# A two-layer graph kernel whose adjacency is turned by VectorE in 32x32 blocks, with half of the row sums added on GpSimd

## The chip, the cores and the metric

The kernel runs on one core of a Trainium2 chip, as one program on the five engines: TensorE (PE, with its weight loads as PEld), VectorE (DVE), ScalarE (ACT), GpSimd (POOL) and SyncE (SP), which here only starts transfers. The metric is the time of one execution on the device in microseconds, as the median of several runs. Everything is computed in fp32.

## What is computed

Two layers work on the same 4096x4096 matrix `adj` and on `x`, 4096x128. Reference, cut:

```python
h = maximum(layernorm(x), 0)
sens = exp(-(1/adj - 1)**2 / 0.5);  weights = where(adj < 1, sens, 0)
x = x + weights @ (h @ W0 + B)                     # layer 0, "acc0"
h = maximum(layernorm(x), 0)
A = adj + eye;  d = sum(A, axis=1) ** -0.5
x = x + relu(d[:, None] * A * d[None, :] @ (h @ W1.T))   # layer 1, "mix"
```

TensorE contracts over the partitions, so both products need the columns of `adj` on partitions, which is the transposed matrix. Layer 1 needs the finished x of all rows, so a block of `adj` whose columns are not known yet has to be stored and used later.

## The kernel before

`adj` is cut into 8 rows of 8 blocks of 512x512 (1 MiB each), 64 units in all. `G = 8` counts rows and columns, `T = 4` tiles of 128. Row by row, each unit goes through these steps (letters are used below):

- **a.** SP loads the block in `raw` (`load`, 4 buffers, one DMA over 128 partitions, runs of 2 KB).
- **b.** TensorE turns it by 16 transposes of 128x128 into PSUM (`turn_tile`, L364), ScalarE copies the result into `kept` in two halves (`copy_half`, L569), and SP stores `kept` in HBM (`store`) where a later use needs it.
- **c.** VectorE sums the raw rows (`row_sum`, L659, 2048 elements a partition).
- **d.** The weights: VectorE `cut` (L673: v*(v<1), one instruction whose two inputs are the same tile in SBUF), ScalarE `log` and `invert` (L574, L580, so that v becomes 1/v), VectorE `quad` (L680: (v-2)*v, again two inputs in SBUF), ScalarE `weigh` (L586: exp).
- **e.** TensorE `multiply_weights` (L381) adds four 128x512 products to `acc0`, three units behind the transposes (`MUL_LAG`).
- **f.** Layer 1: `mix_once` (L397) uses `kept` at once where the block's columns are known, `mix_late` (L420) takes a stored block that GpSimd has loaded back (`load_late`), and what is left comes in an end part (`mix_end_block`, L519, 17 blocks). One such product of a block is four matmuls of 512 columns, 8 records in the profile. Sums that don't fit into PSUM are added to `mixed` in SBUF by VectorE (`add_sum`).

After each row the small chain of that row follows inside the next one: `copy_x1t`, `turn_x1`, `make_x1`, `make_hid`, `turn_hid`, `copy_hid`, `multiply_support`, `make_support`. In the first row the messages (h @ W0 + B) are made between the units. The order on each engine is written out in `turn`, with loops over equal rows (`PHASES`), and the waits are semaphores on counts. The end part finishes eight output rows: `add_end`, `turn_out`, `finish`, a store.

## Time and profile before

| what | value |
|---|---|
| time of the runs | 651.94 us median of 3 (651.78 to 652.38) |
| profiled execution, span | 651.7 us |
| PE, PEld busy | 595.8 us, 337.1 us |
| DVE, ACT, POOL busy | 523.2 us, 479.0 us, 65.2 us |
| bytes moved by DMA | 157.67 MB, mean 242 GB/s |
| granted TensorE clock | 0.988 of full speed |

The span runs from the first to the last instruction of the profiled execution. Busy time is the union of an engine's instructions. An instruction's own duration is a little longer than the distance to the next start when instructions follow each other directly, since their ends overlap; the prediction counts with the distances.

### The profile page before, as it was taken

To read this page: it belongs to the slowest core of one execution; us is meant where nothing else is said; L and a number is where in the kernel's file an instruction comes from. 1 tells how busy PE (TensorE), PEld (TensorE's weight loads), DVE (VectorE), ACT (ScalarE), POOL (GpSimd) and SP (SyncE) were. 2 spreads that over 40 slices of the span, in tenths; PEclk is the share of its full clock that TensorE was granted. 3 is DMA by queue.
4 is the path that set the end of the run, shared out by engine and by line. 5 is a ranking of instruction groups with operands and counts; after the bars stand their busy time and mean duration, and the time that the engine had idled before them with its cause. 6 is when DMAs were issued, how large, how long until landed. Compare 5 with 4: busy or idle time off the path is not lost.

```text
span 651.7 us, 7163 instructions
## 1 busy us (share of the span) xinstructions
PE 595.8 (91%) x2307; PEld 337.1 (52%) x2307; DVE 523.2 (80%) x582; ACT 479.0 (73%) x357; POOL 65.2 (10%) x87
## 2 busy tenths in 40 slices
PE   2498988977979999999999999999999999999995
PEld 2475644544545555655555555554555554444432
DVE  4999999999999999999999994668763868531516
ACT  2799999999999999999999986476484665710000
POOL 2694000000000100010001000100000000001110
PEclk9799999999999999999999999999999999999999
DMA  9987685797886778677678883585744550527983
GB/s 258 388 322 252 236 293 194 263 313 261 271 284 229 253 264 303 252 237 266 223 272 312 300 337 130 186 283 194 268 168 152 202 221 0 205 83 301 301 295 104
DMA packets 54293, 157.67 MB, mean 242 GB/s; under 512 B 2561, under 2 KB 11010, under 8 KB 43778
## 3 DMA queue, kind: packets, MB, share of 16 engines
q1 hardware_dynamic: 48370, 114.43, 50.8%
q0 software_dynamic: 5904, 42.99, 18.0%
q8 instruction: 10, 0.16, 0.1%
q14 instruction: 9, 0.07, 0.0%
HBM read 112.33 MB, written 45.09 MB: 242 GB/s over the span
## 4 chain that ended last, share of the span: by engine, by line
PE 58%; DVE 22%; ACT 8%; issue 8%; DMA 3%; DVEq 0%; SPq 0%; ACTq 0%; POOL 0%; POOLq 0%
PE acc L381 18%; PE acc_late L420 11%; PE acc_once L397 11%; PE turned_ps L364 9%; PE turned_ps L519 6%; DVE rowpart L659 6%; DVE wt L680 5%; DVE wt L673 4%; DMA late<-adj_t_spill 3%; ACT wt L586 2%; PE side L420 2%; ACT wt L580 2%; ACT kept L569 2%; ACT wt L574 2%; DVE msg L779 1%
## 5 line engine op out<-in xcount | busy, mean ns | idle before, releaser
L381 PE MATMUL acc<-wt,msg 128*128 128x512 f32 x512 | 231.8, 596 | 20.4 <-ACT wt L586 20.4
L569 ACT COPY kept<-turned_ps 128x1024 f32<-128x1024 f32 x128 | 124.0, 1027 | 75.5 <-PE turned_ps L364 73.6
L680 DVE SCALAR_TENSOR_TENSOR wt<-wt 128x2048 f32<-128x2048 f32 x64 | 146.3, 2286 | 20.8 <-ACT wt L580 20.7
L381 PEld LDWEIGHTS acc<-wt,msg 128*128 128x128 f32 x512 | 93.8, 190 | 126.9 <-issue 101.9
L659 DVE TENSOR_REDUCE rowpart<-raw 128x4 f32<-128x2048 f32 x64 | 145.8, 2278 | 7.7 <-DMA raw<-in_adj_dram 7.7
L673 DVE SCALAR_TENSOR_TENSOR wt<-kept 128x2048 f32<-128x2048 f32 x64 | 146.2, 2284 | 5.0 <-ACT kept L569 5.0
L364 PEld LDWEIGHTS turned_ps<-ident,raw 128*128 128x128 f32 x1024 | 119.8, 144 | 36.7 <-issue 29.8
L364 PE MATMUL turned_ps<-ident,raw 128*128 128x128 f32 x1024 | 126.9, 279 | 9.6 <-DMA raw<-in_adj_dram 9.4
L586 ACT ACTIVATE wt<-wt 128x2048 f32<-128x2048 f32 x64 | 123.2, 1926 | 15.7 <-DVE wt L680 15.7
L574 ACT ACTIVATE wt<-wt 128x2048 f32<-128x2048 f32 x64 | 124.3, 1943 | 0.1
L580 ACT ACTIVATE wt<-wt 128x2048 f32<-128x2048 f32 x64 | 122.8, 1919 | 0.0
L397 PE MATMUL acc_once<-kept,support 128*128 128x512 f32 x184 | 82.8, 593 | 0.9 <-DVE support L750 0.9
L420 PE MATMUL acc_late<-late,support 128*128 128x512 f32 x160 | 71.7, 593 | 0.0
L519 PE MATMUL turned_ps<-late,support 128*128 128x512 f32 x136 | 61.2, 597 | 1.3 <-DMA late<-adj_t_spill 1.2
L397 PEld LDWEIGHTS acc_once<-kept,support 128*128 128x128 f32 x184 | 33.6, 190 | 37.6 <-issue 37.6
L420 PEld LDWEIGHTS acc_late<-late,support 128*128 128x128 f32 x160 | 29.6, 190 | 33.5 <-issue 33.5
L519 PEld LDWEIGHTS turned_ps<-late,support 128*128 128x128 f32 x136 | 24.8, 190 | 31.1 <-issue 26.3
L304 POOL TENSOR_SCALAR support<-x,mv 128x128 f32<-128x128 f32 x28 | 34.2, 1239 | 17.5 <-DVE support L769 17.5
L311 POOL COPY x<-x_now 128x512 f32 (+1 forms) x8 | 4.9, 612 | 299.1 <-DVE x_now L709 299.1
L835 DVE TENSOR_TENSOR mix_end<-turned_ps,mixed 128x512 f32<-128x512 f32 x8 | 5.5, 691 | 33.1 <-PE turned_ps L519 33.1
L319 POOL DMA_DIRECT2D late<-adj_t_spill x24 | 12.9, 536 | 176.5 <-PE acc_late L420 149.0
L702 DVE COPY x1t<-acc 128x512 f32<-128x512 f32 x8 | 5.5, 684 | 27.0 <-PE acc L381 27.0
(74 smaller groups left out, 216.2 us busy)
## 6 DMA issues: line engine op xcount, KB each, us to landing
raw<-in_adj_dram SPq DMA_DIRECT2D x64, 1024.0 KB, 5.7
adj_t_spill<-kept SPq DMA_DIRECT2D x41, 1024.0 KB, 7.1
late<-adj_t_spill POOLq DMA_DIRECT2D x41, 1024.0 KB, 5.3
x<-in_x_dram SPq DMA_DIRECT2D x4, 512.0 KB, 7.7
out_dram<-fin SPq DMA_DIRECT2D x8, 256.0 KB, 3.2
w_sb<-in_L_gnn_W_dram SPq DMA_DIRECT2D x2, 64.0 KB
b_row<-in_L_gnn_B_dram SPq DMA_DIRECT2D x1, 0.5 KB
```

The lines of the kernel that those rows point to most:

```text
L364: last = nc.tensor.transpose(turned_ps[:, q, a * P:(a + 1) * P], raw[:, p % RAW, a, q * P:(q + 1) * P], ident[:])
L381: mm = nc.tensor.matmul(acc0[:], msg[:, c * T + q, :], wt[:, p % WTS, q, :], start=(p % G == 0 and q == 0), stop=(p % G == G - 1 and q == ...
L397: mm = nc.tensor.matmul(acc_once[:], support[:, c * T + q, :], kept[:, p % KEPT, q, :], start=(begins and q == 0), stop=(ends and q == T - 1))
L420: mm = nc.tensor.matmul(acc[:], support[:, c * T + q, :], late[:, slot, q, :], start=(begins and q == 0), stop=(ends and q == T - 1))
L519: mm = nc.tensor.matmul(turned_ps[:, r % T, :], support[:, c * T + q, :], late[:, slot, q, :], start=((r, c) in begins and q == 0), stop=( ...
L569: nc.scalar.copy(kept[:, p % KEPT, q:q + 2, :], turned_ps[:, q:q + 2, :]).then_inc(copied, 1)
L574: nc.scalar.activation(v, v, ACT.Ln, bias=LN_GUARD).then_inc(ln_done, 1)
L580: nc.scalar.activation(v, v, ACT.Exp, scale=-1.0).then_inc(inv_done, 1)
L586: nc.scalar.activation(v, v, ACT.Exp, scale=-2.0, bias=-2.0).then_inc(wt_done, 1)
L659: nc.vector.tensor_reduce(rowpart[:, :, p:p + 1], raw[:, p % RAW], AX_X, ALU.add).then_inc(summed, 1)
L673: nc.vector.scalar_tensor_tensor(out=wt[:, p % WTS], in0=v, scalar=CUTOFF, in1=v, op0=ALU.is_lt, op1=ALU.mult).then_inc(cut_done, 1)
L680: nc.vector.scalar_tensor_tensor(out=v, in0=v, scalar=-2.0, in1=v, op0=ALU.add, op1=ALU.mult).then_inc(quad_done, 1)
```

## The change

All engine programs are written out over `u` = 0..63 units instead of loops over equal rows, and these parts differ:

- **Turning.** Units come in pairs: one `raw` buffer now holds 2 MiB (two neighbouring blocks), there are 2 buffers, and a pair is loaded by four DMAs of 32 partitions with runs of 1 KB, so that four 32-row groups of `adj` lie on the four quarters of the partitions. VectorE `transpose` turns 32x32 blocks in SBUF, straight from `raw` to `kept`. The 1024 TensorE transposes and the 128 copies of ScalarE go. x and out are read and written in the same permuted order, by DMAs of 32 partitions with runs of 512 B.
- **Row sums.** GpSimd adds the two halves of each run of a pair (`halve`, 2 inputs of 2048 elements a partition), VectorE sums the result, once per pair and not per unit (2048 elements). The parts of a row now lie on four partition quarters, and `sum_quads` (one small matmul) with `own_rows` (two small VectorE instructions) collects them.
- **Squares.** For two units of three ScalarE squares (`square`: (1/v-1)^2, bias -1), for each third (`u % 3 == 1`, 21 units) VectorE does `quad` as before.
- **Layer 1.** Eight PSUM banks are used: each row keeps its own sum in its bank, so the additions to `mixed` go (two rows are moved out by ScalarE in `evict`). 28 blocks are used at once, 20 late in the rows (`JOBS`: 1, 2, 3, 4, 5 and 5 in rows 2 to 7), 16 in the tail. 35 blocks are stored and loaded again where it was 41. In the tail the late blocks have 7 slots, not 3: the freed halves of `raw` serve too.
- **Places.** `copy_x1t` moves from VectorE to ScalarE. `make_x1` stands before the cut of unit 5 of a row, `make_support` before the cut of unit 7; the ScalarE copy that it needs is the last step of unit 6. `cut` follows its own unit's `turn`. `WTS` is 6.

The core of the diff (declarations, the first row's messages and the end are left out):

```diff
+def squared_by_dve(u):
+    return u % 3 == 1
...
+        adj_parts = adj.rearrange("(R e h i) (C q w) -> R h C q i e w", e=16, h=2, i=B, C=C4, q=Q)
...
+            def load(n):
+                g = n // C4
+                if n >= RAW:
+                    sp.wait_ge(halved, n - RAW + 1)
+                    sp.wait_ge(turned, 2 * (n - RAW + 1))
+                for q in range(Q):
+                    sp.dma_start(raw[q * B:(q + 1) * B, n % RAW],
+                                 adj_parts[g // 2, g % 2, col(2 * n) // 2, q]).then_inc(raw_loaded[n % RAW], 16)
...
+            load_x(0)
+            load(0)
...
+            load_x(1)
+            load(1)
+            load_x(2)
+            load_x(3)
+            for u in range(UNITS):
+                if spills(u):
+                    sp.wait_ge(turned, u + 1)
+                    store(u)
+                if u % 2 == 1 and u // 2 + RAW < PAIRS:
+                    load(u // 2 + RAW)
...
+            def halve(n):
+                pool.wait_ge(raw_loaded[n % RAW], 64 * (n // RAW + 1))
+                if n >= 1:
+                    pool.wait_ge(summed, n)
+                nc.gpsimd.tensor_tensor(halves[:], raw[:, n % RAW, :, 0:W // 2], raw[:, n % RAW, :, W // 2:W],
+                                        ALU.add).then_inc(halved, 1)
...
+            for n in range(PAIRS):
+                halve(n)
+                if n < C4 - 1:
+                    make_h0(n + 1)
+                for j in range(len(IN_TURN)):
+                    if load_pair(j) == n:
+                        load_late(j)
...
+            def square(u):
+                v = wt[:, u % WTS]
+                act.wait_ge(inv_done, u + 1)
+                nc.scalar.activation(v, v, ACT.Square, bias=-1.0).then_inc(square_done, 1)
...
+            for u in range(UNITS):
+                g, idx = u // G, u % G
+                log(u)
+                if u >= 1 and not squared_by_dve(u - 1):
+                    square(u - 1)
+                if g >= 1 and idx == 6:
+                    log_pows(g - 1)
+                invert(u)
+                if u >= 1:
+                    weigh(u - 1)
...
+                if g >= 1 and idx == 3:
+                    copy_x1t(g - 1)
...
+                if g >= 1 and idx == 6:
+                    exp_pows(g - 1)
+                    copy_hid(g - 1)
...
+            def turn(u):
+                n, h = u // 2, col(u) % 2
+                if u % 2 == 0:
+                    dve.wait_ge(raw_loaded[n % RAW], 64 * (n // RAW + 1))
...
+                dst = kept[:, u % KEPT].rearrange("p k (e i) -> p e k i", i=B)
+                src = raw[:, n % RAW].rearrange("p e (k h i) -> p e k h i", k=T, h=2)[:, :, :, h, :]
+                nc.vector.transpose(dst, src).then_inc(turned, 1)
+
+            def row_sum(n):
...
+                dve.wait_ge(halved, n + 1)
+                nc.vector.tensor_reduce(dst, src, AX_X, ALU.add).then_inc(summed, 1)
...
+            for u in range(UNITS):
+                g, idx = u // G, u % G
+                turn(u)
+                if g == 0:
+                    cut(u)
+                if idx % 2 == 1:
+                    row_sum(u // 2)
...
+                if g >= 1 and idx == 2:
+                    own_rows(g - 1)
+                if g >= 1 and idx == 5:
+                    make_x1(g - 1)
+                if g >= 1 and idx == 7:
+                    make_support(g - 1)
+                if g >= 1:
+                    cut(u)
+                if u >= 1 and squared_by_dve(u - 1):
+                    quad(u - 1)
```

## Rows read from the trace of the kernel before

**Rows 1.** The page, part 1: busy time of each engine

```profile
PE 595.8 (91%) x2307; PEld 337.1 (52%) x2307; DVE 523.2 (80%) x582; ACT 479.0 (73%) x357; POOL 65.2 (10%) x87
```

**Rows 2.** Windows: stretch and its length, then engines' busy time

```profile
core 0: us, PE busy (x) PEld busy (x) DVE busy (x) ACT busy (x) POOL busy (x), PEclk, DMA share, GB/s
60.00:120.00 60.00, 51.76 (x246) 32.27 (x245) 59.56 (x62) 58.00 (x45) 0.61 (x1) 1.00 0.75 259
360.00:450.00 90.00, 90.00 (x330) 49.15 (x329) 69.40 (x60) 63.87 (x46) 4.84 (x9) 1.00 0.65 233
560.00:651.70 91.70, 82.74 (x225) 37.70 (x223) 34.48 (x86) 11.57 (x9) 9.50 (x18) 0.99 0.64 223
```

**Rows 3.** The chain that ended last, in order of time: start, length, what

```profile
246.68 1.75 PE turned_ps L364 x16
248.43 3.44 PE acc_late L420 x8
...
612.12 8.17 DMA late<-adj_t_spill
```

**Rows 4.** Timeline of DVE: the sum that closes a row (3 of 8)

```profile
72.76 0.19 DVE L665 TENSOR_REDUCE pows<-rowpart 128x4 f32<-128x32 f32 x1
...
375.82 0.18 DVE L665 TENSOR_REDUCE pows<-rowpart 128x4 f32<-128x32 f32 x1
...
556.35 0.19 DVE L665 TENSOR_REDUCE pows<-rowpart 128x4 f32<-128x32 f32 x1
```

**Rows 5.** Timeline of DVE: start, length, instruction; large and small work

```profile
161.32 0.68 DVE L709 TENSOR_TENSOR x_now<-side,x 128x512 f32<-128x512 f32 x1
...
162.82 2.27 DVE L673 SCALAR_TENSOR_TENSOR wt<-kept 128x2048 f32<-128x2048 f32 x1
165.01 0.16 DVE L720 TENSOR_SCALAR pows<-pows 128x4 f32<-128x4 f32 x1
...
166.35 2.28 DVE L680 SCALAR_TENSOR_TENSOR wt<-wt 128x2048 f32<-128x2048 f32 x1
168.55 2.28 DVE L659 TENSOR_REDUCE rowpart<-raw 128x4 f32<-128x2048 f32 x1
170.75 2.28 DVE L673 SCALAR_TENSOR_TENSOR wt<-kept 128x2048 f32<-128x2048 f32 x1
172.95 0.15 DVE L733 TENSOR_TENSOR tmp<-inv 128x8 f32<-128x8 f32 x1
...
175.04 2.28 DVE L680 SCALAR_TENSOR_TENSOR wt<-wt 128x2048 f32<-128x2048 f32 x1
```

**Rows 6.** Timeline of ACT: two instructions that follow each other directly

```profile
304.10 1.92 ACT L574 ACTIVATE wt<-wt 128x2048 f32<-128x2048 f32 x1
305.91 1.91 ACT L586 ACTIVATE wt<-wt 128x2048 f32<-128x2048 f32 x1
```

**Rows 7.** POOL: ns min/median/max of a line; timeline (to 46.5, to 48.4); memsets

```profile
L304 POOL TENSOR_SCALAR support<-x,mv x28: 703/708/2907, 22.6 to 56.1; 128x128 f32<-128x128 f32 x28
44.18 2.91 POOL L304 TENSOR_SCALAR support<-x,mv 128x128 f32<-128x128 f32 x1
...
44.18 4.28 POOL L304 TENSOR_SCALAR support<-x,mv 128x128 f32<-128x128 f32 x3
...
44.23 2.28 DVE L680 SCALAR_TENSOR_TENSOR wt<-wt 128x2048 f32<-128x2048 f32 x1
L296 POOL MEMSET mixed<- 128x2048 f32 x1 | 1.8, 1797 | 0.0
L298 POOL MEMSET mixed<- 128x512 f32 x1 | 0.5, 517 | 0.0
```

**Rows 8.** Start: DVE's first instruction in the timeline, and a window

```profile
7.73 2.29 DVE L659 TENSOR_REDUCE rowpart<-raw 128x4 f32<-128x2048 f32 x1 [7.73 <-DMA raw<-in_adj_dram]
22.00:40.00 18.00, 11.12 (x57) 8.73 (x56) 17.90 (x19) 17.49 (x17) 17.36 (x15) 0.81 1.00 373
```

**Rows 9.** Timeline of DVE: the addition behind the last block

```profile
643.73 0.69 DVE L835 TENSOR_TENSOR mix_end<-turned_ps,mixed 128x512 f32<-128x512 f32 x1 [0.54 <-PE turned_ps L519]
```

More of the change, by code:

```diff
@@ L83 @@
-class Turn:
-    def __init__(self, first, w, known):
-        self.first, self.w, self.known = first, w, known
-        self.row = first + w
-    def blocks(self, p, per=1):
-        return (self.first * G + p) * per + self.w * (G * per)
-    def tally(self, events, p=0):
-        before = sum(sum(events(k)) * n for f, n, k in PHASES if f < self.first)
-        return before + self.w * sum(events(self.known)) + sum(events(self.known)[:p])
+C4 = 4
+Q = 4
+B = 32
+T = 4
+RAW, KEPT, WTS, LATE = 2, 4, 6, 3
@@ new lines, with col, at_once, spills @@
+LAG = 3
+PAIRS = G * C4
+UNITS = 2 * PAIRS
+ORDER = [[0, 1, 2, 3, 4, 5, 6, 7]]
+for turn_row in range(1, G):
+    young = turn_row - 1
+    ORDER.append([c for c in range(G) if c // 2 != young // 2] + [young ^ 1, young])
+def col(u):
+    return ORDER[u // G][u % G]
+def at_once(u):
+    return col(u) < u // G
+def spills(u):
+    return col(u) >= u // G and (u // G, col(u)) != (G - 1, G - 1)
+def spill_count(u):
+    return sum(spills(v) for v in range(u % KEPT, u + 1, KEPT))
+def once_count(u):
+    return sum(at_once(v) for v in range(u + 1))
@@ L178, in build @@
         inv_done = sem("inv_done")
+        square_done = sem("square_done")
         quad_done = sem("quad_done")
@@ L261, in turn @@
-            def turn(t, last=False):
-                for p in range(G):
-                    if not (last and p + AHEAD >= G):
-                        load(t, p + AHEAD, t.first * G + p + AHEAD)
-                    if stored(t.known)[p]:
-                        store(t, p)
-            sp.dma_start(w0_sb[:], w0).then_inc(w_loaded, 16)
-            sp.dma_start(w1_sb[:], w1).then_inc(w_loaded, 16)
-            sp.dma_start(b_row[:], b0.rearrange("(a d) -> a d", a=1)).then_inc(w_loaded, 16)
-            first = Turn(0, 0, 0)
@@ L289, in _ @@
+            for i in range(2):
+                sp.wait_ge(out_written[i], 64 * (G // 2))
         @block.gpsimd
@@ L536, in _ @@
[L536 to L552 removed]
+            ended = 0
@@ L614, in turn, with copy_hid @@
[L614 to L635 removed]
+            def copy_hid(g):
+                act.wait_ge(hid_turned, g + 1)
+                nc.scalar.copy(hid_t[:], side[:]).then_inc(hid_t_done, 1)
@@ L648, in _ @@
+            square(UNITS - 1)
+            weigh(UNITS - 1)
+            copy_x1t(G - 1)
             log_pows(G - 1)
@@ new lines, in make_quads @@
+            def make_quads():
+                dve.wait_ge(ident_done, 1)
+                quads = ident[:].rearrange("p (q i) -> p q i", q=Q)
+                for q in range(Q):
+                    nc.vector.tensor_reduce(quad_sum[:, q], ident[:].rearrange("p (q i) -> p i q", q=Q), AX_X, ALU.add)
+                for a in range(T):
+                    for c in range(C4):
+                        last = nc.vector.tensor_reduce(own_quad[:, a, :, c:c + 1], quads, AX_X, ALU.add)
+                last.then_inc(quads_done, 2)
@@ L838, in finish @@
[L838 to L853 removed]
+            take_moments(0)
@@ new lines, in _, with finish @@
+            own_rows(G - 1)
+            make_x1(G - 1)
+            make_support(G - 1)
+            def finish(i):
+                r = ENDS[i]
+                rows = slice(r * T, r * T + T)
+                dve.wait_ge(mix_turned, i + 1)
+                if i >= 2:
+                    dve.wait_ge(out_written[i % 2], 64 * (i // 2))
+                nc.vector.tensor_tensor(fin[i % 2], tail_bank[r][:].rearrange("p (a d) -> p a d", a=T),
+                                        support[:, rows, :], ALU.add).then_inc(out_summed, 1)
+                dve.wait_ge(out_summed, i + 1)
+                for a in range(T):
+                    last = nc.vector.tensor_scalar(fin[i % 2][:, a, :], fin[i % 2][:, a, :],
```

902 lines of the change are left out of this document (394 added, 508 removed), and 10 rows, old and new, of tables (JOBS, LATE).

## The prediction

> **What bounds the kernel now.** I read the busy times of the page first. TensorE is busy for 91% of the span, VectorE for 80%, ScalarE for 73% [rows 1]. Shares over a whole span hide the stages, so I read the windows next. In the stretch 60 to 120 VectorE is busy 59.6 of 60 us, ScalarE 58.0 and TensorE 51.8; from 360 to 450 TensorE alone is full, and behind 560 the others have little left [rows 2]. So there are two regimes. The row ends show them in time: five rows from 72.76 to 375.82 take 303.1 us, 60.6 each; what follows takes 275.9 us to the end of the span [rows 4]. In the first regime VectorE and ScalarE set the pace together, in the second TensorE does, with its blocks following each other at 3.44 us and the turns at 1.75 us [rows 3]. The chain also has waits for late blocks in the tail, two of about 8 us, of which one is shown [rows 3].
>
> The reader should see what follows from that: removing TensorE work pays from row 6 on, and only there. In rows 1 to 5 the turns are not on the bound of TensorE, but their replacement is put on VectorE, which has nothing free.
>
> **TensorE, rows 6, 7 and tail.** Removed: 64 turns of 1.75 us, 112 us in all, though only those behind 375.82 are on the path [rows 3]. What stays from the start of row 6: 8 weight blocks, 6 at once, 5 late; then 8, 7 and 5; then 3 and 16. That is 19 + 20 + 19 = 58 blocks, and 58 x 3.44 = 199.5 us. Three small chains add two groups of four transposes and four products each, at the transposes' pace (1.75 for 16) some 2 us a chain: 6. Eight output turns at the same pace and a wait each, 3.5. The last weights come late by ScalarE's work on the last unit: I allow 5 us. Behind the last block stand the addition, an output turn, the finish and the store as now; that takes from 643.7 to 651.7, 8.0 us [rows 9]. Sum 222 us, against 275.9 now. The two late-block waits of 8 us are gone in it, since 7 slots let loads run ahead: a block of 1.05 MB at the 373 GB/s of a full window takes 2.8 us [rows 8], less than the 3.44 it serves. If that cover fails, up to 16 us come back.
>
> **VectorE, rows 1 to 5.** Large instructions of 2048 elements start 2.20 us apart: 166.35, 168.55, 170.75, 172.95 [rows 5]. Before, a row has 8 sums, 8 cuts and 8 quads. After, it has 8 turns, 8 cuts, 4 sums and 21/8 quads: 22.6 x 2.20 = 49.8 us, not 52.8. The trace has no VectorE transpose. Its nearest rows are the one-input sum and the two-input cut, both with 2048 elements and both at 2.28 us [rows 5]; one pass at 2.20 is what I take. Below that I see no case, since no instruction of this size is faster. The other bound is two passes, 4.4 us.
>
> Small work: the three stretches 161.32 to 162.82, 165.01 to 166.35 and 172.95 to 175.04 sum to 4.9 us [rows 5] and stay. The copy and the additions go; `own_rows` (0.5) and the wait of each cut for the turn right ahead of it (0.5) come: 5.9.
>
> A new wait: `make_support` now stands before the cut of unit 7, and needs the last step of ScalarE's unit 6. After the cut of unit 6 ScalarE has log, square, invert and weigh, 4 x 1.81 [rows 6], two small activations and the copy, about 8.3; TensorE's products take 1 more. VectorE has only a turn, a sum and 1 us of small steps, 5.4. It waits some 3.5 us a row, with unit 7's cut behind it and ScalarE's next log behind that. Together 49.8 + 5.9 + 3.5 = 59.2 us a row, about what it is now (60.6): two thirds of the squares have paid for the turns. ScalarE, at 29.4 activations a row by 1.81 and 2 us of small ones, has 55, and is not the bound. TensorE has as few as 9 blocks in row 1, and the granted clock was 0.81 where it was busy 11.1 of 18 us [rows 8]; even at the lower of its two levels, 1.2 GHz, 9 blocks take 62 us, so this costs nothing there.
>
> **GpSimd's additions.** This decides. In the trace GpSimd's short instruction takes 703 ns as a rule and 2907 at most; the one at 44.18 needs 2.91 us, and stands beside VectorE's two-input quad of 44.23 to 46.51 [rows 7]. So they use something together, and GpSimd waited. The trace has no long GpSimd instruction, so the opposite, a cut waiting for an addition, is not shown. The addition's own time is unknown too. A memset passes an element in (1797 - 517) / 1536 = 0.83 ns [rows 7]. If its three streams (two in, one out) all overlap, the addition takes 1.8 us; if they follow each other, 5.2. I take 4.3, between two and three streams one after another. (The 703 ns for 128 elements, scaled, would give 11 us, but the memset of 512 takes 517, so most of it is fixed.)
>
> The placement: `halve(n)` starts when the sum of pair n-1 is done. Beside it the cut starts first; the addition follows, and runs through the next turn, which has one input. After 2.3 us comes the next cut and has to wait 2.0 us. For the pair of unit 1 `own_rows` hides 0.5: 1.5. At unit 5 `make_x1` (about 3.7 us with its waits) leaves 0.6. At unit 7 it lies in the 3.5 us above. Where a quad follows the cut, in one pair of three, it may lose 4.3 instead of 2.0: 0.7 a row. Together 4.8, so a row takes 64.0 us and five take 320. Bounds: 0 if the addition takes under 2.3 us, and 7.8 a row at 5.2 us.
>
> The Trainium skill (SBUF — State Buffer, Who interferes with whom) says that a VectorE instruction with two SBUF inputs and a GpSimd instruction that reads SBUF exclude each other for the whole instruction, and that the later one blocks fully. The row at 44.18 agrees for GpSimd as the later one. With that rule the sum is the one made here, without it the first rival's. The same notes (GPSIMD Engine Reference, Elementwise — side-by-side cycle accounting) measured 4497 ns for such an addition; by it a row would be 0.7 us longer, and the sum 4 us.
>
> POOL's queue also holds `make_h0` and the late loads. A late load waits for a block that TensorE finished some five units earlier, so it doesn't hold the next `halve`.
>
> **Row 0.** Before, VectorE starts at 7.73 with one MiB landed [rows 8]. After, 1 MiB of x and 2 MiB of a pair come first: at 373 GB/s 5.6 us more than one block, 13.3; at half that rate 22. I take 15. From 7.73 to 72.76 were 65.0 us with 22 large instructions; there are 22 again (8 turns, 8 cuts, 4 sums, 2 quads). The messages stay. Added: 20 small reductions of `make_quads` 5, GpSimd's additions 4 x 2.0 = 8, the last cut 2. Row 0 ends at 95; now about 75.
>
> **Sum.** 95 + 320 + 222 = 637. In rows 5 to 7 VectorE (64), and TensorE (17, 19 and 20 blocks, 60 to 71 us) are close to each other, and where two paces meet both lose a little: 2 us a row, 6. **643 us**. The span of 651.7 is 0.2 under the median of the runs, 651.94, so nothing is added. About 49 us are won behind row 5 and about 39 lost before. What lies within 0.2% (1.3 us) can't be told from no change.
>
> **Rivals.**
>
> 1. *GpSimd doesn't hold VectorE up* (the addition is short, or only GpSimd ever waits). Rows of 59.2, row 0 at 87: 87 + 296 + 222 + 6 = **611**. For it: the only blocked engine in the trace is GpSimd. Against it: a thing used by two is seldom given back in the middle.
>
> 2. *The loads become the bound; slower.* A DMA now reaches 32 partitions in place of 128, with runs half as long. A row moves 15 MiB: at 373 GB/s 42 us, hidden. If the 8.39 MB of raw go at half that rate, 44.9 + 19.7 = 64.6 us a row, level with VectorE, and with two buffers only both wait for each other; at 5% more a row is 68. Then 20 more in rows 1 to 5, 8 in row 0 and 4 behind: **675**. It decides where raw falls under some 185 GB/s. Against it: the trace has no DMA of 32 partitions. The Trainium skill (SBUF — State Buffer, Door 1: The DMA port swizzle) says that 32 partitions reach 8 of 16 ports and measured 189 GB/s; a row would take 64.1 us by it, so it speaks for this rival. No row here shows it.
>
> 3. *The addition stops all of VectorE*, turns too: three pairs a row lose 4.3 and not 1.6. Rows of 72, also in rows 6 and 7; 105 + 360 + 227 + 6 = **698**. Against it: behind the quad, beside VectorE's one-input sum, GpSimd's next two took (4.28 - 2.91) / 2 = 0.7 us each, undisturbed [rows 7].
>
> 4. *The turn takes two passes.* 59.2 + 17.6 = 77 a row, over GpSimd's addition and over TensorE in all of rows 1 to 7: 105 + 539 + a tail of 84 = **728**.
>
> **How the numbers follow.** The forecast's case 0.45, its own range 625 to 662 (addition from 3.5 to 5.2 us, first load from 13 to 22): 0.28 of it faster, 0.05 the same, 0.12 slower. Rival 1 0.25, faster. Rival 2 0.17, rival 3 0.07, rival 4 0.06, all slower. Faster 0.53, same 0.05, slower 0.42. The range 604 to 692 leaves out rivals 3 and 4 and the edges of the rest.
>
> **What the profile after would show.** The turn at 2.3 us by 64. GpSimd's addition at 4 to 5 us by 32, and cuts behind it of 4 us where the rest take 2.3; only 2.3 everywhere means rival 1. A wait of VectorE for TensorE's products of some 3 us a row at `make_support`. Waits for `raw` on VectorE's turn only in row 0; in every pair they mean rival 2. Row ends 64 us apart until row 5, then 68 to 73. TensorE busy about 470 us. What would make it wrong most easily is the two-engine conflict, worth 32 us between its ends, and the loads.

## The result, and the profile after

The changed kernel takes **693.84 us** (median of 4 runs, 688.3 to 694.83) against 651.86 for the kernel before on the same chip: ratio 1.063, 95% interval 1.059 to 1.067. It is slower by 42 us; the forecast was 643, a gain of 1.4%, and its range ended at 692.

The page, part 1 answers to [rows 1]. TensorE lost 79 us of work, VectorE gained 14, GpSimd 147; nobody is above 78%:

```profile
PE 516.6 (75%) x1299; PEld 245.0 (35%) x1299; DVE 537.4 (78%) x579; ACT 450.9 (65%) x294; POOL 212.6 (31%) x98
```

The windows answer to [rows 2]. The first is row 1 (without its first turn, which starts at 94.7), the second rows 2 to 5 (without row 5's last quad), the third rows 6 and 7, the last the tail:

```profile
core 0: us, PE busy (x) PEld busy (x) DVE busy (x) ACT busy (x) POOL busy (x), PEclk, DMA share, GB/s
97.00:172.00 75.00, 35.02 (x83) 15.99 (x82) 64.20 (x49) 49.91 (x31) 23.99 (x8) 0.78 1.00 266
172.00:459.00 287.00, 217.41 (x508) 99.33 (x507) 245.84 (x196) 219.82 (x134) 91.91 (x24) 0.86 0.84 213
459.00:607.00 148.00, 142.16 (x352) 63.78 (x352) 119.77 (x99) 109.56 (x68) 45.06 (x18) 0.99 0.67 178
607.00:693.00 86.00, 78.36 (x220) 37.02 (x218) 24.99 (x77) 16.02 (x16) 6.83 (x13) 0.97 0.52 183
```

Before, VectorE was busy 59.6 of 60 us in the matching stage [rows 2]. Now it is busy 245.8 of 287, ScalarE 219.8 and TensorE 217.4: **no engine is full in rows 2 to 5**. Behind row 5 TensorE is full, as forecast. To size the stages I take the start of `make_support` (L757), which the timeline gives once a row. Two of the eight close the stages:

```profile
168.91 1.13 DVE L757 TENSOR_SCALAR support<-side,scale 128x128 f32<-128x128 f32 x4
...
455.69 1.13 DVE L757 TENSOR_SCALAR support<-side,scale 128x128 f32<-128x128 f32 x4 [1.84 <-PE side L443]
```

I put it 3.4 us ahead of a row's end, so the forecast's sum reads 95 + 64 - 3.4 = 155.6, then 4 x 64 = 256, then 231.4. (It is 3.2 in row 1 and 5.4 in row 5, where a quad follows; with these two the last column reads 13, 33 and 4.)

| stage (by L757) | forecast | measured | off by |
|---|---|---|---|
| start to row 1 | 155.6 | 168.9 | +13 |
| rows 2 to 5 | 256.0 | 286.8 | +31 |
| row 6 to the end | 231.4 | 237.3 | +6 |

Where does VectorE stand still in rows 2 to 5? The waits of DVE in 172 to 459 (us in total, times, longest), and what ScalarE waits for there:

```profile
DVE tmp L661 <- ACT inv L570: 15.6, 4, 5.8
DVE x L729 <- PE side L431: 14.6, 4, 5.9
DVE wt L657 <- ACT wt L530: 5.3, 4, 1.6
DVE support L757 <- PE side L443: 4.2, 3, 1.8
...
ACT wt L525 <- DVE wt L651: 76.3, 15, 16.6
```

VectorE waits 39.7 us for ScalarE and TensorE, 9.9 a row. ScalarE waits 76.3 for VectorE; of this the longest wait, 16.6, began in row 1 at 155.6, so some 60 belong to rows 2 to 5, 15 a row. Each waits for the other. The chain of waits around one row shows how (start, length, what):

```profile
271.63 1.91 ACT wt L525
273.54 1.80 ACT wt L535
275.34 1.80 ACT wt L530
277.14 1.80 ACT wt L544
278.94 0.48 ACT x1t L562
...
279.56 6.39 PE acc L393 x8
285.95 0.45 PE side L431 x4
286.42 0.70 DVE x L729
...
289.50 2.19 DVE wt L651
```

A cut ends, ScalarE does four large steps and the small copy, TensorE a weight block and four transposes, and only then can VectorE begin `make_x1`, 14.8 us after the chain's start. The next cut is queued behind `make_x1` and starts at 289.50, 17.9 us after the chain's start, and ScalarE's next logarithm waits 5.1 us for it. Beside the chain VectorE does two turns, a cut and a sum, to 282.5; then it stands still for the 3.9 us that are left. TensorE's block takes 6.39 us there. Timeline of PE, and the window of that block (granted clock 0.57, near the lower level of 1.2 GHz, behind 11.1 us of idling):

```profile
279.56 6.39 PE L393 MATMUL acc<-wt,msg 128*128 128x512 f32 x8 [11.10 <-ACT x1t L562]
...
286.22 3.60 PE L393 MATMUL acc<-wt,msg 128*128 128x512 f32 x8
```

```profile
279.50:286.00 6.50, 6.44 (x10) 2.85 (x11) 3.04 (x2) 6.50 (x4) 3.32 (x1) 0.57 1.06 359
```

The next block takes 3.60 us, at a granted clock of 1.00 (286.2 to 289.8).

The second loss is the read conflict. Timeline of DVE (answers to [rows 5]) and of POOL, around one addition:

```profile
199.02 2.28 DVE L651 SCALAR_TENSOR_TENSOR wt<-kept 128x2048 f32<-128x2048 f32 x1
201.21 2.31 DVE L635 STREAM_TRANSPOSE kept<-raw 128x2048 f32<-128x2048 f32 x1
203.55 4.29 DVE L651 SCALAR_TENSOR_TENSOR wt<-kept 128x2048 f32<-128x2048 f32 x1
```

```profile
199.24 6.45 POOL L328 TENSOR_TENSOR halves<-raw 128x2048 f32<-128x2048 f32 x1 [11.47 <-DVE rowpart L644]
214.58 4.52 POOL L328 TENSOR_TENSOR halves<-raw 128x2048 f32<-128x2048 f32 x1 [8.89 <-DVE rowpart L644]
```

The addition of 199.24 stood behind the cut of 199.02 and shows 6.45 us; without a cut ahead of it an addition takes 4.5 (214.58). The turn passes beside it in 2.31, and the next cut, which shows 4.29 us, waits 2.0. That is the forecast's picture to a tenth.

The third loss is in row 1. Timeline of POOL:

```profile
119.61 6.31 POOL L328 TENSOR_TENSOR halves<-raw 128x2048 f32<-128x2048 f32 x1 [6.82 <-DMA raw<-in_adj_dram]
125.86 1.30 POOL L350 DMA_DIRECT2D late<-adj_t_spill  x2
156.57 0.53 POOL L350 DMA_DIRECT2D late<-adj_t_spill  x1 [29.41 <-DMA adj_t_spill<-kept]
157.11 4.51 POOL L328 TENSOR_TENSOR halves<-raw 128x2048 f32<-128x2048 f32 x1
```

The third late load asks for unit 14, whose store isn't even issued when GpSimd reaches it. GpSimd stands 29.4 us in it, with the addition of the next pair queued behind. VectorE's sum waits 9.4 us for that addition, and ScalarE stands 16.6 us, over the same time, until VectorE's next cut is done.

### The profile page after: what moved, and what is told of

Its sections match the earlier page's. It is cut to its first block, busy times and chain, and to the rows that moved or that the text cites. A ratio compares the mean times of both kernels' runs of the same rounds, so it can differ in the third digit from the quotient of the medians.

```text
span 693.0 us, 4089 instructions
## 1 busy us (share of the span) xinstructions
PE 516.6 (75%) x1299; PEld 245.0 (35%) x1299; DVE 537.4 (78%) x579; ACT 450.9 (65%) x294; POOL 212.6 (31%) x98
## 4 chain that ended last, share of the span: by engine, by line
PE 30%; DVE 30%; ACT 20%; issue 12%; DMA 5%; POOL 2%; SPq 1%; DVEq 0%; POOLq 0%
PE mix L415 10%; PE acc L393 10%; DVE wt L651 8%; DVE kept L635 7%; ACT wt L525 5%; PE mix L406 5%; ACT wt L530 5%; ACT wt L535 4%; DVE wt L657 4%; ACT wt L544 4%; DMA raw<-in_adj_dram 3%; DVE rowpart L644 2%; POOL halves L328 2%; DMA late<-adj_t_spill 2%; PE acc L415 1%
## 5 line engine op out<-in xcount | busy, mean ns | idle before, releaser
L393 PE MATMUL acc<-wt,msg 128*128 128x512 f32 x512 | 250.1, 637 | 68.7 <-ACT x1t L562 66.5
L328 POOL TENSOR_TENSOR halves<-raw 128x2048 f32<-128x2048 f32 x32 | 171.7, 5364 | 333.4 <-DVE rowpart L644 310.3
L525 ACT ACTIVATE wt<-wt 128x2048 f32<-128x2048 f32 x64 | 121.9, 1905 | 134.0 <-DVE wt L651 133.7
L635 DVE STREAM_TRANSPOSE kept<-raw 128x2048 f32<-128x2048 f32 x64 | 147.4, 2303 | 7.4 <-DMA raw<-in_adj_dram 7.4
L530 ACT ACTIVATE wt<-wt 128x2048 f32<-128x2048 f32 x64 | 121.6, 1900 | 0.6
L406 PE MATMUL mix<-kept,support 128*128 128x512 f32 x224 | 104.0, 609 | 12.0 <-DVE support L757 8.4
L415 PE MATMUL mix<-late,support 128*128 128x512 f32 x200 | 92.4, 606 | 3.1 <-DMA late<-adj_t_spill 3.1
L544 ACT ACTIVATE wt<-wt 128x2048 f32<-128x2048 f32 x43 | 81.5, 1895 | 0.0
L535 ACT ACTIVATE wt<-wt 128x2048 f32<-128x2048 f32 x43 | 81.4, 1894 | 0.0
L644 DVE TENSOR_REDUCE rowpart<-halves 128x16 f32<-128x2048 f32 x32 | 72.0, 2250 | 9.4 <-POOL halves L328 9.4
L657 DVE SCALAR_TENSOR_TENSOR wt<-wt 128x2048 f32<-128x2048 f32 x21 | 69.2, 3296 | 8.4 <-ACT wt L530 8.4
L406 PEld LDWEIGHTS mix<-kept,support 128*128 128x128 f32 x224 | 42.7, 195 | 65.2 <-issue 60.1
L415 PEld LDWEIGHTS mix<-late,support 128*128 128x128 f32 x200 | 38.7, 196 | 52.9 <-issue 47.5
L541 ACT ACTIVATE wt<-wt 128x2048 f32<-128x2048 f32 x21 | 39.8, 1898 | 15.4 <-DVE wt L657 15.4
```

The costliest lines, as they stand in the source:

```text
L328: nc.gpsimd.tensor_tensor(halves[:], raw[:, n % RAW, :, 0:W // 2], raw[:, n % RAW, :, W // 2:W], ALU.add).then_inc(halved, 1)
L393: mm = nc.tensor.matmul(acc0[:], msg[:, col(u) * T + k, :], wt[:, u % WTS, k, :], start=(first and k == 0), stop=(last and k == T - 1))
L406: mm = nc.tensor.matmul(once_bank[g][:], support[:, c * T + k, :], kept[:, u % KEPT, k, :], start=(first and k == 0), stop=False)
L415: mm = nc.tensor.matmul(bank[:], support[:, c * T + k, :], late_tile(slot)[:, k, :], start=(start and k == 0), stop=(stop and k == T - 1))
L525: nc.scalar.activation(v, v, ACT.Ln, bias=LN_GUARD).then_inc(ln_done, 1)
L530: nc.scalar.activation(v, v, ACT.Exp, scale=-1.0).then_inc(inv_done, 1)
```

## The experiments

All times are medians beside runs of the kernel before on the same chip (651.9 to 652.6 us). "Row" is a mean over rows 2 to 5, from one `make_support` to another.

### First batch: which part of the change costs

**e1_no_add.** GpSimd doesn't add, and VectorE sums the first half of each run, so the row sums lack the second halves. VectorE then no longer waits for anything that GpSimd does to a pair, so this run also takes away the wait of row 1 shown above.

```diff
-                nc.gpsimd.tensor_tensor(halves[:], raw[..., 0:W // 2], raw[..., W // 2:W], ALU.add)
...
-                src = halves[:]...
-                dve.wait_ge(halved, n + 1)
+                src = raw[:, n % RAW, :, 0:W // 2]...
```

> GpSimd's 32 additions are left out, and VectorE's sum reads the first half of each run of raw as it lies, so the row sums lack the other half; every wait of the queue stays. Two theories for the 50 us over the forecast. 'Port': the additions and VectorE's two-input instructions exclude each other; cuts lose 16.6 us over the whole run (2543 against 2284 ns by 64), quads 21.2 (3296 against 2286 ns by 21), small ones about 10, and what lies in rows 0 to 5 comes back: about 650 to 658 us, every cut and quad at 2.28. 'Places': the small chain's steps stand where one engine waits for another, and the additions only fill time that is idle anyway: 683 to 692 us, with VectorE's waits at make_x1 and make_support grown by what the cuts give back.

**e2_write_only.** In place of the addition three memsets of GpSimd fill the same tile (2.5 times 2048 elements, about 4.6 us); row sums as in e1.

> As the run without additions, but GpSimd writes for about 4.4 us in their place (three memsets of 2.5 x 2048 elements to a tile that nobody reads), so it is as busy and reads nothing. 'Port' as a matter of the read side: cuts stay at 2.28 and the time is that of the run without additions. If what is shared is the whole port pair, or GpSimd's being busy at all, cuts behind it take 4.3 us again and the time is near 690.

**e4_cut_first.** `make_x1` and `make_support` stand behind the unit's cut and quad.

```diff
-                if g >= 1 and idx == 5: make_x1(g - 1)
-                if g >= 1 and idx == 7: make_support(g - 1)
                 if g >= 1: cut(u)
                 if u >= 1 and squared_by_dve(u - 1): quad(u - 1)
+                if g >= 1 and idx == 5: make_x1(g - 1)
+                if g >= 1 and idx == 7: make_support(g - 1)
```

> make_x1 and make_support stand behind the cut and the quad of their unit, nothing else changes. 'Places': ScalarE gets its next log before VectorE waits for the small chain; VectorE waited 14.6 us at make_x1 and 19.8 us at make_support in four rows, 8.6 us a row, and ScalarE 76 us for cuts. Most of 6 rows x 8.6 comes back: 645 to 665 us. 'Port' alone: 688 to 695 us.

**e6_copy_sooner.** ScalarE's `copy_x1t` one unit earlier (`idx == 2`, was 3).

> ScalarE's copy_x1t stands at the end of unit 2 of a row and not of unit 3. If the late x1t is what TensorE (19 us idle a row) and then make_x1 (3.65 us a row) wait for, TensorE idles some 7 us less a row, make_x1 doesn't wait, and 15 to 25 us come back: 669 to 679 us. If the order on VectorE alone is to blame, 688 to 695 us.

| kernel | us | ratio to before, 95% |
|---|---|---|
| changed kernel | 693.84 | 1.059 to 1.067 |
| e1_no_add | 658.96 | 1.007 to 1.012 |
| e2_write_only | 665.48 | 1.015 to 1.021 |
| e4_cut_first | 680.44 | 1.040 to 1.044 |
| e6_copy_sooner | 687.71 | 1.048 to 1.056 |

Leaving the additions out gives 34.9 us: 18.5 up to row 1's `make_support`, 13.7 in rows 2 to 5, 3.8 behind. The first of these contains row 1's wait for GpSimd's queue, which e5 below prices at 7. The places give 13 us (e4), where 29 to 49 were expected, and 6 (e6), where 15 to 25 were. The groups by line show that it is GpSimd's reading that holds cut and quad (busy, mean ns); first after, then e2:

```profile
L651 DVE SCALAR_TENSOR_TENSOR wt<-kept 128x2048 f32<-128x2048 f32 x64 | 162.8, 2543 | 1.0
...
L657 DVE SCALAR_TENSOR_TENSOR wt<-wt 128x2048 f32<-128x2048 f32 x21 | 69.2, 3296 | 8.4 <-ACT wt L530 8.4
```

```profile
L655 DVE SCALAR_TENSOR_TENSOR wt<-kept 128x2048 f32<-128x2048 f32 x64 | 146.3, 2287 | 1.0
...
L661 DVE SCALAR_TENSOR_TENSOR wt<-wt 128x2048 f32<-128x2048 f32 x21 | 48.1, 2290 | 16.1 <-ACT wt L535 16.1
```

With 4.6 us of writes per pair on GpSimd, cut and quad keep their 2.29 us. e2 is still 6.5 us slower than e1. Up to row 5 the two run level (424.6 and 423.5 at `make_support`), and the rest lies behind it; why, no run shows. Yet without any addition the kernel is still not faster than before, so the additions can't be the whole.

### Second batch: the places together, with and without the additions

**e5_late_later.** The first three late loads are issued after the additions of pairs 6, 7 and 8, and not all after that of pair 6 (`units[0] // 2 - 2 + j` for `units[0] // 2 - 2`).

> The first three late loads are issued after the additions of pairs 6, 7 and 8, not all after pair 6. In the changed kernel GpSimd waits 29.4 us there for the store of unit 14, with the addition of pair 7 behind it, while VectorE waits 9.4 us for that addition and ScalarE 16.6 us for a cut. If that queue is what made row 1 longer than the others, 12 to 18 us come back, 676 to 682 us, all of it before the make_support of row 1 (168.9 us). If the wait for raw behind it (halve waited 16 us for a pair) would have taken over, under 4 us: 690 to 694.

**e8_all_order.** e4, e5 and e6 together.

> Three changes of place at once: make_x1 and make_support behind cut and quad, copy_x1t a unit sooner, the first late loads later. Alone the first gave 13 us and the second 6. If they are three separate waits: 693 - 13 - 6 - 15 = 655 to 662 us. If the sooner copy and the cut first pay for the same wait, 663 to 670. The additions' price stays (quads at 4.2 us behind the small chain).

**e9_order_no_add.** e8 and e1 together (row sums lack the second halves).

> The three changes of place and no additions (row sums over the first half only, so half of the row sum is left out). Without additions the kernel took 659 us, with rows of 67 to 71 us where the work of VectorE is 56 and of ScalarE 55. If places are the rest, rows come to 57 to 60 us and the time to 615 to 625 us. If the two engines can't run beside each other for another reason (one unit of slack between cut, log and quad), rows stay over 63 and the time over 640.

**e10_order_sq_act.** e8, and ScalarE takes all 64 squares (`squared_by_dve` is never true).

> The three changes of place, with the additions, and all 64 squares on ScalarE. VectorE loses 21 quads (48 us alone, 69 to 90 with the additions' waits), ScalarE gets 21 activations (38 us, rows of 60). 'Port': the quads are where the additions cost most (3.3 to 4.3 us against 2.3), and VectorE's lead over ScalarE grows: under 650 us, 630 to 648. 'ScalarE becomes the bound': rows of 64 and more, 655 to 670 us.

| kernel | us | ratio to before, 95% |
|---|---|---|
| e5_late_later | 687.52 | 1.049 to 1.056 |
| e8_all_order | 672.85 | 1.030 to 1.035 |
| e9_order_no_add | 632.17 | 0.967 to 0.976 |
| e10_order_sq_act | 638.21 | 0.977 to 0.983 |

Three of these four results missed what I expected. e5 gave 6 us and not 12 to 18. e8 is slower than both its cases. e9 lies between its two. Only e10 came as one of its cases said.

Now the rows can be taken apart. Waits are those of DVE in rows 2 to 5. "Held" is what instructions of VectorE take over their undisturbed length; for after, the 33 cuts at 2576 ns over 2287, the 11 quads at 3157 over 2290, and two small lines, 25.3 us in all; for e8 the same lines, the quads at 4652 ns alone being 26 of 50 us. "Rest" is what is left.

| kernel | row | waits | held | rest |
|---|---|---|---|---|
| forecast | 64.0 | 3.5 | 4.8 | 55.7 |
| after | 71.7 | 9.9 | 6.3 | 55.5 |
| e1 (no additions) | 68.3 | 13.2 | 0 | 55.1 |
| e8 (places) | 68.6 | 0.3 | 12.5 | 55.8 |
| e9 (both) | 62.7 | 6.8 | 0 | 55.9 |

This table is the finding. The rest is the same in each, within 0.8 us, and is what the forecast said. **Waits and conflicts hide each other**: without additions half of what they held turns into waiting for ScalarE and TensorE; without the waits the quads run straight into the additions. e4 alone already brings the row to 68.7. In rows 2 to 5 the sooner copy and the later loads add nothing to it; their share of e8 lies in row 1. Of e9's waits 2.4 a row are for `raw`. The waits of DVE in rows 2 to 5, e1 and then e8:

```profile
DVE x L726 <- PE side L429: 16.6, 4, 6.8
DVE tmp L658 <- ACT inv L568: 15.6, 4, 5.8
DVE wt L654 <- ACT wt L528: 10.9, 8, 1.7
DVE support L754 <- PE side L441: 9.1, 5, 1.8
```

```profile
DVE tmp L661 <- ACT inv L570: 1.0, 1, 1.0
```

and a quad of e8 that stands behind an addition (timelines of POOL and of DVE):

```profile
222.35 6.44 POOL L328 TENSOR_TENSOR halves<-raw 128x2048 f32<-128x2048 f32 x1 [9.39 <-DVE rowpart L644]
```

```profile
224.31 6.63 DVE L657 SCALAR_TENSOR_TENSOR wt<-wt 128x2048 f32<-128x2048 f32 x1
```

So one part alone undersells: over the kernel the additions cost 34.9 us with the waits in place and 40.7 without them (e8 to e9), although e8 has no wait for GpSimd's queue left in row 1. The squares cost 34.6 on top of e8, 15.7 of them up to row 1. In rows 2 to 5 a row loses 5.8 us of quads and their 6.5 us of holding, yet falls only by 5.2, to 63.4, since the waits rise from 0.3 to 8.0: ScalarE with 32 activations of 1.81 us and some small ones, 60 us, is now the fullest engine (busy 236 of 253 us).

### Third batch: the loads

**e12_before_32.** The kernel before, each raw block loaded by four DMAs of 32 partitions, in the same 2 KB runs.

```diff
-                sp.dma_start(raw[:, p % RAW], adj_blocks[...]).then_inc(raw_loaded[p % RAW], 16)
+                for i in range(4):
+                    part = slice(i * 32, (i + 1) * 32)
+                    sp.dma_start(raw[part, p % RAW], adj_blocks[..., part]).then_inc(raw_loaded[p % RAW], 16)
```

> The kernel before, and only its raw block of 1 MiB comes by four DMAs of 32 partitions (runs of 2 KB kept) in place of one of 128. It shows what the narrow transfers cost by themselves. If 32 partitions go at about half the rate (second rival of the prediction), a block takes 8 us or more from issue to landing where it was 5.7, a row's 8.4 MB of raw alone need some 45 us, and with 19.7 for the rest a row of 60.6 becomes 64 or more: 665 to 680 us. If the four narrow DMAs side by side fill the engines as one wide does, the time stays at 650 to 656.

**e13_wide_loads** and **e14_order_sq_wide.** The changed kernel, and e10, with the four DMAs of a pair over 128 partitions each; `adj` then lies wrongly on the partitions.

```diff
-                    sp.dma_start(raw[q * B:(q + 1) * B, n % RAW], adj_parts[g // 2, g % 2, col(2 * n) // 2, q])
+                    sp.dma_start(raw[:, n % RAW, 4 * q:4 * q + 4], adj_wide[g, col(2 * n) // 2, q])
```

> The changed kernel with each of a pair's four raw DMAs over 128 partitions in place of 32: same bytes, same number of DMAs, same 1 KB runs, but the rows of adj then lie wrongly on the partitions, so the output is not the reference's. If the narrow loads took part in the 71.8 us of a row (second rival), the rows fall by 4 us or more and the time to 670 or less, with DMA's share well under 1.0 in rows 1 to 4. If only additions and places cost, as the first two batches suggest, only row 1 gains something (the store that GpSimd waited 29 us for lands sooner): 685 to 694.

> As e13, on top of e10 (three steps placed later or sooner, all squares on ScalarE; 638.2 us): wide raw loads, the output is not the reference's. In e10 GpSimd waits 127 us for raw, so the loads are nearer to the bound. If they bound there, the rows of 61 to 62 us fall toward ScalarE's 58 to 60 and the time to 620 to 630; if ScalarE (8 x 4 x 1.81 = 58 us a row and 2 us of small ones) is the bound, it stays at 634 to 639.

**e11_order_sq_full.** e10 without GpSimd's additions, VectorE sums all 4096 elements of a pair.

> As e10 (all squares on ScalarE, three steps placed differently), but GpSimd adds nothing and VectorE sums the whole run of 4096 elements for a pair. VectorE then has 8 turns, 8 cuts and 4 sums of twice the length: 24 x 2.2 = 53 us and 6 of small work, 59 a row, against 20 x 2.2 + 6 + the additions' price (2 us x 4) = 58 with GpSimd. If the additions' price is as large as 35 to 41 us over the kernel, as measured, this gives about the same or a little less than e10's 638.2: 630 to 640. If the additions pay for themselves once the quads are gone, it is 642 to 650.

| kernel | us | ratio to before, 95% |
|---|---|---|
| e12_before_32 | 656.40 | 1.004 to 1.007 |
| e13_wide_loads | 677.25 | 1.035 to 1.045 |
| e14_order_sq_wide | 627.05 | 0.957 to 0.962 |
| e11_order_sq_full | 640.92 | 0.977 to 0.986 |

I had expected 685 to 694 of e13; it gave 17 us, and e14 another 11 on e10. So the width of a load does cost. Size, number and runs of the DMAs are the same, but with the width the rows of `adj` that one DMA reads change too, and no run parts these two. The DMA view of 172 to 240 in 40 slices (busy share in tenths, rate), first of after, then of e13:

```profile
DMA  3193398999999809979999999979999996799999
GB/s 62 48 414 154 159 352 148 258 218 222 215 216 323 357 0 366 231 189 234 204 222 210 233 395 410 361 192 211 206 223 207 275 347 219 142 261 208 221 209 189
```

```profile
DMA  8999307709989999208999999200699900000000
GB/s 177 383 358 346 101 0 304 313 0 352 217 269 377 348 384 426 96 0 337 222 272 378 348 380 420 111 0 0 155 364 372 333 14 0 0 10 0 0 0 0
```

A 9 is a slice in which the DMA engines count as busy for 90% or more. After has 29 of them, and 18 move only 189 to 234 GB/s; e13 has 18, of which 15 move 333 or more, and in the end it has nothing left to move. Stores and late blocks lie among them. The Trainium skill (SBUF — State Buffer, Door 1: The DMA port swizzle) gives 189 GB/s for partitions 0 to 31, and some 218 as the limit. Eleven of the 18 slices lie between these two, seven above, at 221 to 234, so the trace agrees roughly.

Where do the 17 us of e13 fall? `make_support` of rows 1 and 5 starts at 158.73 and 440.88: 10.2 us come in rows 0 and 1, 4.6 in rows 2 to 5, the rest behind. VectorE hardly waited for raw in after (7.4 us, all at the start); what came late were stores (6.4 us to land, 5.3 in e13) and late blocks (7.8, and 5.4), which share the engines with raw. The wait of GpSimd for the store of unit 14 falls from 29.4 to 22.1, and VectorE's for the addition behind it from 9.4 to 2.2. In the kernel before the same narrowing cost 4 us only, where 13 or more were expected at half the rate: DMA's share in rows 1 to 5 rose from 0.76 to 0.93. I take it that the four buffers hid the rest; no run varies their number. Nor does one vary the length of the runs, 2 KB before and 1 KB after.

e11 against e10 is 640.9 to 638.2 with intervals that overlap: once the quads are gone, adding on GpSimd buys nothing that can be measured over summing everything on VectorE.

### Fourth batch: everything at once, and one part by itself

**e16_all_off.** e9 with the wide loads of e13: no additions, moved places, wide loads (both departures from the data named there).

> The changed kernel without GpSimd's additions (row sums lack their second halves), with the three places moved, and with raw loads over 128 partitions (adj lies wrongly): all three found causes taken away at once; the output is not the reference's. If they are all of it, the time comes near the 611 us that the prediction gave for a kernel where GpSimd holds nothing up: 608 to 618. If something else holds rows 1 to 5 as well (VectorE and ScalarE passing a unit back and forth, TensorE at its lower clock), the loads give back what they gave in e14, 11 us, or less: 619 to 630.

**e7_squares_act.** The changed kernel, all squares on ScalarE, nothing else.

```diff
 def squared_by_dve(u):
-    return u % 3 == 1
+    return u < 0
```

> The changed kernel, and only the 21 squares of VectorE go to ScalarE. On top of the moved places this gave 34.6 us. If a quad costs its own 2.2 us, its wait of up to 2 us behind an addition and the handing over with ScalarE's invert, whatever the places, this gives 25 to 40 us alone: 654 to 669. If the gain needs the moved places (because VectorE then only waits longer at make_x1 and make_support), it is under 15: 679 or more.

**e15_best_wide.** e10 with wide loads that put the data right: 16 DMAs a pair, one for each group of rows.

```diff
-                for q in range(Q):
-                    sp.dma_start(raw[q * B:(q + 1) * B, n % RAW], adj_parts[g // 2, g % 2, col(2 * n) // 2, q])
+                for e in range(16):
+                    sp.dma_start(raw[:, n % RAW, e], adj_parts[g // 2, g % 2, col(2 * n) // 2, :, :, e])
```

> As e10 (638.2 us), with a pair loaded by 16 DMAs of 128 KB over all 128 partitions, each with one of the 16 row groups, in place of 4 over 32 partitions: the data lie as they should. If the width of the transfer was what cost in e10, this gives what e14 gave: 624 to 630. If many small transfers cost as much again as the width gains, it stays at 636 or more.

| kernel | us | ratio to before, 95% |
|---|---|---|
| e16_all_off | 620.76 | 0.950 to 0.954 |
| e7_squares_act | 683.66 | 1.045 to 1.050 |
| e15_best_wide | 970.57 | 1.486 to 1.491 |

e16 closes most of the account. Its `make_support` starts at 141.89 in row 1 and 386.75 in row 5: a row is 61.2, waits 5.4, rest 55.8. The forecast's case without interference had 59.2 a row, 3.5 of it waits. Taking all three away gains 27.0 us up to row 1, 41.9 in rows 2 to 5, 2.6 behind. The 2 us a row that remain are waits, most of them of VectorE's quads for ScalarE (DVE, then ACT, rows 2 to 5 of e16):

```profile
DVE wt L655 <- ACT wt L529: 16.5, 5, 9.4
...
ACT x1t L561 <- PE acc L392: 8.8, 2, 7.2
```

The longest, 9.4 us in row 5, comes behind ScalarE's wait of 7.2 us for TensorE.

e7 shows the same hiding again: 10.2 us for the squares alone, where they gave 34.6 on top of e8. VectorE's waits in rows 2 to 5 rise from 39.7 to 68.9 us. My 25 to 40 was wrong, the theory that the gain needs the moved places was right in kind.

e15 went to 970.6 for another reason. Timeline of SP (its queue; start, length, count of issues):

```profile
302.36 23.42 SPq L280 DMA_DIRECT2D raw<-in_adj_dram  x15
```

15 issues take 23.4 us, 1.56 each, so a pair takes 25 us to issue: 32 pairs, 800 us. The DMA engines are busy only 0.41 of the time (150 to 500), so the issuing holds the loads back and not the moving. VectorE waits 341.8 us for raw. It says nothing about the width.

### Fifth batch: can the width be had with the right data?

**e17_sq_act_q_order.** e10, the four DMAs of a pair in the order 0, 2, 1, 3 of the partition quarters.

> As e10 (638.2 us), and the four raw DMAs of a pair are issued for the partition quarters 0, 2, 1, 3 in place of 0, 1, 2, 3. If DMAs of one queue overlap enough, and quarters 0 and 2 are served side by side where 0 and 1 are not, the rate in the windows rises over 220 GB/s and some of e14's 11 us come: 627 to 634. If each DMA of a queue is done before the next has its bytes moved, nothing changes: 636 to 640.

**e18_sq_act_two_queues.** e10, quarters 2 and 3 issued on GpSimd's queue, ahead of the late loads.

```diff
+            def load_rest(n):
+                if n >= RAW:
+                    pool.wait_ge(halved, n - RAW + 1)
+                    pool.wait_ge(turned, 2 * (n - RAW + 1))
+                for q in (2, 3):
+                    pool.dma_start(raw[q * B:(q + 1) * B, n % RAW], adj_parts[...]).then_inc(raw_rest[n % RAW], 16)
...
             for n in range(PAIRS):
                 halve(n)
+                if n + RAW < PAIRS:
+                    load_rest(n + RAW)
```

> As e10, with the quarters 2 and 3 of each pair issued on GpSimd's queue and 0 and 1 on SP's, so that DMAs for partitions 0 to 63 and 64 to 127 run at one time. If the reach of one DMA is the limit, both together move 350 to 400 GB/s and e14's 11 us come back with the right data: 625 to 631. If what the transfers read (1 KB pieces 16 KB apart for one quarter) is the limit, or GpSimd's issuing holds its additions up, it stays at 636 or goes over it.

| kernel | us | ratio to before, 95% |
|---|---|---|
| e17_sq_act_q_order | 634.95 | 0.972 to 0.977 |
| e18_sq_act_two_queues | 707.54 | 1.082 to 1.086 |

In 97 to 172 both move 298 GB/s, e10 300: neither the order nor a second queue raises the rate. e17 gives 3 us, its interval and e10's just don't overlap. e18 is much slower, because GpSimd's queue now holds more (waits of POOL, then of PE's weight loads):

```profile
POOL raw L346 <- DVE kept L651: 263.4, 28, 30.9
...
PEld mix L430 <- DMA late<-adj_t_spill: 66.3, 6, 18.6
```

GpSimd stands 263 us before its raw loads, until VectorE has turned the buffer's last unit. The late blocks are queued behind that and take 12.6 us to land (7.6 in e10), and TensorE waits 66 us for them, nearly all of it behind row 5. There too lies e18's loss: its rows 2 to 5 take 62.0 us each (e10 63.4), what follows 305 us where e10 has 235. No run separates the shares of these waits.

**e17_sq_act_q_order, at 634.95 us, is the fastest version that leaves nothing out**: 2.6% below the kernel before and 8.5% below the changed one.

## Why the prediction was wrong

The forecast was 643, measured are 693.8. By its own steps:

- **TensorE's part behind row 5** (222, with 6 for handing over): right to 6 us, 237.3 against 231.4. **Row 0** ended at 94.7 (forecast 95), with some luck: the first turn started at 17.7 and not at 15, and the additions held less than the 8 us put down for them. The 13 us that are missing up to row 1 are all row 1's, see below. **The turn** at one pass of 2.28: right, 2303 ns in 64. **GpSimd's addition** taken as 4.3 us: 4.5. **A cut behind it** waits 2.0: 2.0 measured. The remaining large and small work, 55.7 a row: 55.5. Rival 1 (nothing holds VectorE), rival 3 (all of VectorE stops) and rival 4 (two passes) are out: cuts show 4.29 us, turns 2303 ns.
- **The step that failed: "It waits some 3.5 us a row", at `make_support` alone.** Measured are 9.9, at three places: 5.0 at `make_support` with the Newton step ahead of it, 3.7 at `make_x1`, and 1.3 at the quad that needs the inverse of the unit just before. I had checked the hand-over only at unit 7, where I had asked who would be late; the same question at unit 5 gives the chain shown above, 14.8 us to `make_x1`, of which VectorE's own work covers 11. e8 shows that the places make these waits: with the two steps behind cut and quad, and the copy sooner, they are 0.3. This term is 6.4 a row too low, 26 us of the 31 missing in rows 2 to 5. That is its size in the sum and not what mending it gives: e8's row is only 3.1 us shorter, since the held time rises by 6.2.
- **The additions' term, 4.8 a row**: 6.3 measured. The mechanism was right for cut and quad (e1, e2: only the reading holds them). Their 4.8 is met exactly, but by luck: forecast were 4.1 for cuts and 0.7 for quads, measured are 2.4 and 2.4. The 1.5 that are missing are two small instructions, of which I had counted none. One is the Newton step, which has two inputs. The other, `hid` in `make_x1`, reads one tensor of 128 elements a partition (and a scalar a partition from `mv`), so it isn't only two-input instructions that are held. Four of them take 0.88 us undisturbed; in e8, beside an addition, 3.10:

```profile
210.01 3.10 DVE L741 TENSOR_SCALAR hid<-x,mv 128x128 f32<-128x128 f32 x4
```

  The term isn't stable either: 12.5 once the waits are gone. (The row at 44.18 was a weaker witness than I made it: GpSimd's record starts 0.05 us before the quad's, and yet GpSimd is the one that was held.)
- **"It doesn't hold the next `halve`"**: false for the first three late loads. They are all issued behind pair 6, and one asks for unit 14, of the same stage. It stands in the row-1 fence: 29.4 us on GpSimd, 9.4 on VectorE, 16.6 on ScalarE. e5 takes VectorE's wait away, and row 1's `make_support` starts 7 us sooner (161.93 for 168.91).
- **"Even at the lower of its two levels ... this costs nothing there"**: false. I compared TensorE's whole load of a row with the row. But one block of `multiply_weights` lies between ScalarE's last step and `make_x1`, and behind the idle time it took 6.39 us and not 3.44 [rows 3], 3 us on the path. No run here varies the clock alone, so that share is read from the chain, not shown by an experiment. TensorE was busy for 516.6 us and not the 470 of the forecast; its granted clock was 0.78 in row 1 and 0.86 in rows 2 to 5.
- **Rival 2, loads**: I gave 0.17 to rows of 68 with the loads as bound. They weren't the bound, but e13 puts their share at 17 us, mostly in rows 0 and 1, where stores and late blocks land later. As all-or-nothing it was the wrong question.
- **Two thirds of the squares "have paid for the turns"**: in counts of instructions, yes, in time no. Squares that stay on VectorE meet the additions and the hand-over. With them on ScalarE and the places moved the kernel is 14 us faster than before, not 42 slower (e10).

The causes overlap, so their sizes alone (35, 21, 17, 10 us) don't sum to anything meaningful; all but the squares taken away together give 73 (e16). 621 against the 611 of rival 1 stays: 8 us of it are the 2 us a row of waits in rows 2 to 5, and 3.4 lie behind row 5, which stay open.

## What to carry to other kernels

When work moves between engines that pass each unit back and forth, don't sum busy times: at every place where one engine's small step stands ahead of its large ones, write down what it waits for, how long that chain is, and what is queued behind. Three places in the order, which cost nothing in code, were worth 21 us here, and they decide what other changes are worth: the same squares gave 10 or 35. Move one thing in two settings before you price it.

## What was unexpected of the hardware

- A two-input instruction of VectorE and a reading one of GpSimd hold each other up in both directions: the cut 2.28 to 4.29 us, the addition 4.5 to 6.45. Three GpSimd writes of 4.6 us do nothing to it (2287 ns). The Trainium skill (SBUF — State Buffer, Who interferes with whom) says just this, that such a VectorE instruction does not contend with a GpSimd instruction that only writes; e2 agrees.
- An instruction of VectorE with one input tensor can be held too, even by writes. `hid` took 3.10 us beside an addition (e8) and 1.81 beside the memsets of 194.57 and 196.43 (e2), where four of them take 0.88 undisturbed:

```profile
195.74 1.81 DVE L745 TENSOR_SCALAR hid<-x,mv 128x128 f32<-128x128 f32 x4
```

- A tiny instruction pays the whole price. The Newton step of 0.17 us in row 1 of after:

```profile
164.25 4.35 DVE L666 SCALAR_TENSOR_TENSOR inv<-tmp,inv 128x8 f32<-128x8 f32 x1
```

- With loads over 32 partitions, 18 of the 29 slices in which the DMA engines count as busy move 189 to 234 GB/s; with loads over 128, 15 of 18 move 333 or more. Another order of the quarters or a second queue left the rate at 298 GB/s (97 to 172), where it was 300.
- Small transfers of pieces far apart (128 KB each) cost SP's queue 1.56 us an issue, back to back, while the DMA engines were busy 0.41 of the time (e15).
